# Three kinds of work in ScalarE's hand-written step, in another order

## What is computed

```python
xn  = layernorm(x)
gnn = segment_sum(edge_weight[:, None] * xn[src], dst, 6250) @ Wg + bg      # 100000 edges
q   = elu(xn @ Wq + bq) + 1                                                  # 8 heads of 64
k   = elu(xn @ Wk + bk) + 1
v   = xn @ Wv + bv
kv  = sum over rows of k^T v, per head;  z = 1 / (q . sum over rows of k)
mix = (q kv z) @ Wp + bp
x   = x + gnn + mix
out = x + ffn(layernorm(x))       # gate of eight task vectors, two products, layernorm
```

## Time and profile before

| | us |
|---|---|
| median of 3 runs (lowest, highest) | 1786.94 (1784.66, 1795.36) |
| the profiled execution | 1800.53 |
| its span, first to last instruction | 1798.6 |
| PE busy | 1496.3 (83%) |
| DVE busy | 998.8 (56%) |
| POOL busy | 858.1 (48%) |
| ACT busy | 649.3 (36%) |
| mean clock granted to PE | 0.915 of full speed |

### The profile page before, as it was taken

The page is one execution under the profiler, slowest core; times in us unless marked ns, Lnnn a source line. Parts: engine busy times, 40 slices in busy tenths (PEclk is TensorE's granted clock), DMA queues, the critical chain, the costliest instruction groups (busy, mean ns, idle before and its releaser), DMA issues. The chain is left out here.

```text
span 1798.6 us, 25809 instructions
## 1 busy us (share of the span) xinstructions
PE 1496.3 (83%) x8355; PEld 645.4 (36%) x8355; DVE 998.8 (56%) x2041; ACT 649.3 (36%) x1045; POOL 858.1 (48%) x882
## 2 busy tenths in 40 slices
PE   4988778788879886968879888888798699998995
PEld 2544323333323333323333333333333344463332
DVE  7878323333333433335655546676767766545877
ACT  4877411222222221022323223233323477624543
POOL 0003366666666666366666666665656254500000
PEclk9999889889989998588988988999999799999997
DMA  6898677777777777366666666666666644535774
GB/s 226 305 328 289 227 220 236 224 232 231 238 219 239 234 223 249 104 195 198 200 198 200 201 194 200 198 198 200 194 193 182 192 167 162 207 123 169 240 251 151
DMA packets 163921, 379.33 MB, mean 211 GB/s; under 512 B 26924, under 2 KB 32702, under 8 KB 163808
## 3 DMA queue, kind: packets, MB, share of 16 engines
q0 software_dynamic: 62720, 205.57, 39.0%
q1 hardware_dynamic: 100368, 171.27, 28.1%
q10 hardware_dynamic: 720, 1.06, 0.2%
HBM read 300.77 MB, written 78.23 MB: 211 GB/s over the span
## 5 line engine op out<-in xcount | busy, mean ns | idle before, releaser
L1143 POOL DMA_INDIRECT rows<-y_rows,idxT x516 | 496.4, 962 | 312.9 <-issue 149.4
L910 ACT ACTIVATE mb<-bank,ones,ncols 128x512 f32<-128x512 f32 x98 | 76.2, 778 | 586.9 <-remote 320.6
L1476 DVE SCALAR_TENSOR_TENSOR acc<-bank,maskt,acc 128x512 f32 x196 | 138.1, 746 | 143.6 <-remote 83.1
L2008 PE MATMUL bank<-xr,kh 128*128 128x512 f16 x392 | 134.5, 428 | 43.3 <-issue 24.6
L1926 PE MATMUL bank<-KVP,qT 128*128 128x512 f16 x588 | 151.2, 404 | 13.2 <-issue 12.5
L2024 PE MATMUL bank<-rows,hots 128*32 128x512 f16 x1548 | 130.0, 409 | 31.9 <-issue 27.8
L1926 PE MATMUL bank<-Wg,xtb 128*128 128x512 f16 x588 | 139.8, 389 | 18.1 <-DVE xtb L1410 9.0
L1926 PE MATMUL bank<-Wq,xta 128*128 128x512 f16 x588 | 151.8, 413 | 0.0
L1926 PE MATMUL bank<-Wk,xta 128*128 128x512 f16 x588 | 143.3, 392 | 7.3 <-issue 7.3
L2036 PE MATMUL bank<-part,plc 128*128 128x512 f32 x196 | 119.0, 687 | 27.0 <-issue 21.4
L1926 PE MATMUL bank<-ztg,G 128*128 128x512 f16 (+1 forms) x624 | 135.6, 370 | 0.0
(11 more groups left out here) (313 smaller groups left out, 2482.7 us busy)
## 6 DMA issues: line engine op xcount, KB each, us to landing
xta<-xt_rows SPq DMA_DIRECT2D x98, 256.0 KB
x_rows<-xhl SPq DMA_DIRECT2D x49, 256.0 KB, 3.6
xt_rows<-xtb SPq DMA_DIRECT2D x49, 256.0 KB, 3.9
y_rows<-yb SPq DMA_DIRECT2D x49, 256.0 KB, 3.7
xr<-x_rows SPq DMA_DIRECT2D x49, 256.0 KB
z_rows<-zn SPq DMA_DIRECT2D x49, 256.0 KB, 2.0
zt_rows<-ztg SPq DMA_DIRECT2D x49, 256.0 KB, 2.0
zq<-z_rows SPq DMA_DIRECT2D x49, 256.0 KB, 2.7
```

Source lines behind the costliest of these rows:

```text
L910: nc.scalar.activation(mb[:, :], of[:, :], ACT.Relu, scale=ncols[:, col:col + 1], bias=ones[:, 0:1]).then_inc(f_min, 1)
L1143: pool.indirect_dma_start(out=row_slot(s, k).rearrange("p a d -> p (a d)"), out_offset=None, in_=y_rows, in_offset=bass.IndirectOffsetOnAx ...
L1476: nc.vector.scalar_tensor_tensor(out=flat(acc, tile + m), in0=edge_bank(n)[:, :], scalar=maskt[:, m, n:n + 1], in1=flat(acc, tile + m), op ...
L2008: ins = nc.tensor.matmul(bank[c][:, :], (kh, kl)[p][:, b, s], xr[:, b, q, :], start=isinstance(t, int) and t == 0 and i == 0, stop=isinsta ...
```

## The change

In each step ACT first makes the high parts (of the tiles two steps back), then copies the partial sum, and then makes the features (of the tile one step back); before, the features came first, then the high parts, then the copy. The steps in which each piece of work is done stay as they were, and so do the lists of all other engines.

```diff
@@ -950,9 +950,8 @@
             act.wait_ge(y_low, T)
             act.wait_ge(pool_set, 20)
             for s in range(K_FIRST, SLOTS_END):
-                for slot_of, after, work in ((k_slot, 1, k_feature), (q_slot, 1, q_feature), (k_slot, 2, k_higher),
-                                             (q_slot, 2, q_higher)):
-                    t = tile_of(slot_of, s - after)
+                for slot_of, work in ((k_slot, k_higher), (q_slot, q_higher)):
+                    t = tile_of(slot_of, s - 2)
                     if t is not None:
                         work(t)
                 if s == TURN + 1:
@@ -962,6 +961,10 @@
                 if s == TURN + 4:
                     kv_rows()
                 keep_part(s)
+                for slot_of, work in ((k_slot, k_feature), (q_slot, q_feature)):
+                    t = tile_of(slot_of, s - 1)
+                    if t is not None:
+                        work(t)
                 t = tile_of(q_slot, s - 3)
                 if t is not None:
                     q_outward(t)
```

## The result

| | before | changed |
|---|---|---|
| median of 9 runs, us (lowest, highest) | 1786.64 (1777.69, 1795.36) | 1794.95 (1785.40, 1801.37) |
| ratio of the times, 95% interval | | 1.0057 (1.0030 to 1.0084) |
| the profiled execution, us | 1800.53 | 1799.75 |

The change costs 8 us; forecast were 7 us gained. The range (1744 to 1824) holds the time, the sign is wrong. The two profiled executions are equally long, so their difference in total says nothing; what follows goes by stages, each read from several profiles.

The account below looks back on a forecast made before the run. The prediction took PE to set the pace, with POOL's gathers as the next bound. Keys 40 us gained (39 + 8 - 7) and queries 33 us lost gave -7 us, from a median of 1786.9 to 1780 us, range 1744 to 1824.

Parts of the forecast that it names:

- Part 1: Keys: `kh` ahead of the pair's second feature ends PE's wait before `m_product`; 39 us gained plus about 8 us of clock.
- part 2: Keys: features behind the copy wait for the step's sums when it ends a group; 7 us lost.
- Part 3: Queries: features behind the copy delay the low part and PE's turn in 37 of 49 tiles; 33 us lost.
- Part 4: Queries: the earlier copy gains almost nothing and `q_outward`, at most 1.4 us later, costs nothing; counted as zero.
- A: Rival, slower: queries lose their full 59 us, keys gain only 20; sum +39, 1826 us; chance 0.25.
- B: Rival, faster: keys gain 55 us, near POOL's bound, queries lose only 15; sum -40, 1747 us; chance 0.25.
- POOL's bound: Keys: gathers take 5.0 us a slot, so the keys can't become shorter than 405 us, a gain of 70.
- C: Rival, prompt releases: keys gain 24 us, queries lose at most 3; sum -21, 1766 us; chance 0.06.
- D: Rival, nothing changes: each wait removed on ACT is found again behind another engine; 1787 us; chance 0.04.

Follow-up runs that it names:

- three_gathers: Kernel before with three gathers of rows instead of four in each slot below 74 (sums wrong), prompt chip: ratio 0.9777 to the kernel before, median 1578.6 us.
- late_queries_only: Kernel before with the changed order only for query features of steps 148 and later, prompt chip: ratio 1.0061 to the kernel before.
- three_all_changed: Changed kernel with three gathers instead of four in all slots, late chip: 0.8877 of the kernel before, 17 us slower than the old order with three gathers.
- outward_ahead: Changed kernel with `q_outward` moved right behind the copy of the partial sum, ahead of the features, late chip: ratio 1.0096 to the kernel before.
- before_b: Kernel before, unchanged, run again for a second profile on a late chip: ratio 1.0008 to itself.
- after_b: Changed kernel, unaltered, run a third time, on a late chip: ratio 1.0013 to the kernel before.

## Why the prediction was wrong

**What bounds the kernel: wrong, and with it the sums.** I took PE for the bound because its 393 us of busy time filled most of 475. But busy time at a clock of 0.92 isn't need: the same matmuls take 350 us when nothing holds PE up (three_gathers). On the prompt chip POOL sets the pace among the keys, 5.05 us a slot, which I had only as a far limit. On late chips the pace is 5.8 to 6.0 us a slot; it depends on how many gathers a slot has (half the bytes change nothing, one gather fewer does), though POOL's own 5.0 us lie below it. What links the two there is open.

**Part 1, 40 us gained with part 2: the step that failed.** `m_product`'s idle fell from 43.0 us to 7.8, below the 10 named, and the stretch shrank by 6 us in that pair of profiles and by 0.5 on the average of all on late chips. By the forecast's own words (less than 20 us although `m_product` no longer waits) part 1 is wrong. I had counted a wait taken away as time gained. On late chips PE's idle from slot 0 to 81 fell only from 79-82 us (three profiles with the old order) to 66-76 (five with the high part first), 10 us on average; before `krows` it rose from 4-10 to 6-26. And these 10 us went into PE's busy time, 392 us before and 402 after on average, since its time at half the clock rose from 55-72 us to 79-99. I had booked 8 us of gain from less of it. Why it rose isn't shown. On the prompt chip the gathers took it all.

**Part 3, 33 us lost: the right direction, the wrong size and a wrong argument.** Forecast for `turn_q`'s idle was about 70 us; it was 72 to 102. But the queries' stretch grew by 2 us in the first pair and by 8 on the average of the four late profiles with the new order (649.5 against 641.1). In the first pair `turn_q` took 52 us more, while PE's other stands fell by 36 us, not by 6, and its busy time by 14. On the prompt chip 20 of the 37 tiles carry all of it (late_queries_only). That a gather fewer uncovers a loss at the others too is seen in three_all_changed, on a late chip. The argument that a late turn delays the next product too, which then has more time, fails for tiles two steps apart: there the next product stands ahead of the turn (1010.80 before 1015.12 above), and what the late turn delays is the next feature, through the sums and the copy.

**Part 4, nothing: right for `q_outward`,** since outward_ahead gave nothing back. The earlier copy by itself was not tested; `place` stands 17 us less in the first pair of profiles and 9 less in the second (before_b, after_b).

**Rivals.** A had the sign and two of its reasons, the third product as the next to wait and the half clock, but 39 us where 8 came. B expected the keys to gain 55 us, close to POOL's bound; they gained none. C's condition, prompt releases, exists on one chip; its result, 21 us gained, doesn't: 24 of keys' gain needs three gathers to show, and the queries lose 10, not 3. C took the room before a turn, 9.52 us, from the earlier trace rows; on the prompt chip PE comes to the turns that wait after 6.2 to 7.3 us. D had the reason for the keys, a wait that is found again elsewhere. In 161 releases on the prompt chip the semaphore comes 0.01 to 0.03 us after the modelled end. The sentence of the Trainium skill that I quoted (Perfetto Trace Analysis, section Tensor Engine Instruction) fits this chip. The rows of the late ones don't refute it as I said they do: it speaks of the write, and the rows have only a modelled end.

**Open** stays what makes PE's releases late on some chips while gathers are issued, why a wait taken away there doesn't come back as time, and where the changed kernel's 8 us of the first comparison are spent. With four gathers no order beat the kernel before by more than it differs from itself.

## What to carry to other kernels

A wait that is removed is worth its length only if nothing else sets the pace: take the suspected next bound away (one gather fewer) and see whether the gain appears, before adding up idle times. Divide the stage's time by its units; if it comes out nearly the same (5.8 to 6.0 us a slot here) for stretches with different work, suspect that the work you are looking at doesn't make the pace. And when a step is put behind another engine's result in a list, compare the longer chain with the least time that the waiting engine has, not with one example (6.2 us here before some turns, 11.3 before a neighbour). Look also whether that result itself waits for the step one round earlier: then a delay is handed on to the next round, and costs something only where that round has no room.

## What the hardware showed that I had not expected

- The same program takes 1610 us on one chip and 1783 to 1797 on others, with its head equally long (first sums at 219 to 224 us on both) and its tail too (396 to 405 us on late chips, 399 to 408 on the prompt one); the difference is made while gathers run.
- On the late chips the gathered rows lie ready a median 14 to 15 us before their sums among the keys, by the DMA packets' records, on the prompt one 1.9 us: by those records it isn't the data that PE waits for there.
- On late chips half the rows per gather give no gain (1.007), and one gather fewer in four gives 12% (0.878).
- PE's busy time for the same matmuls is 350 us at a granted clock of 1.00 and 393 at 0.92.
